# Gated cross-attention stack: the first attention's probabilities turned by VectorE and two DRAM passes instead of by TensorE

## The reference, cut to what matters

```python
q_hk = (hidden_q @ Wq.T).reshape(b, s, H, K)
q_big = jnp.einsum('bshk,hkq->bshq', q_hk, w_kc_q)
kv_rope = kv_c * cos[None] + _rotate_half(kv_c) * sin[None]
q_r = jnp.einsum('bshq,hqr->bhsr', q_big, W_qr)
k_r = jnp.einsum('bld,hdr->bhlr', kv_rope, W_kr)
scores = jnp.einsum('bhsr,bhlr->bhsl', q_r, k_r)
attn = jax.nn.softmax(scores, axis=-1)
ctx_c = jnp.einsum('bhsl,bld->bhsd', attn, kv_rope)
ctx_lat = jnp.einsum('bhsd,hkd->bshk', ctx_c, w_kc_kv)
out = ctx_lat.reshape(b, s, H * K) @ Wo.T
```

## Time and profile before

| what | value |
|---|---|
| median of 3 runs | 1410.36 us (1408.68 to 1412.06) |
| profiled execution, its own time | 1410.01 us |
| its span | 1408.2 us |
| mean granted TensorE clock | 0.998 of full speed |
| PE busy | 1384.4 us, 98% of the span |
| PE weight loads busy | 1128.5 us, 80% |
| DVE busy | 874.9 us, 62% |
| ACT busy | 519.2 us, 37% |
| POOL busy | 404.9 us, 29% |
| DMA moved | 89.07 MB, mean 63 GB/s |

### The profile page before, as it was taken

How to read it: one execution, slowest core, us unless ns; L and a number is a source line. 1 busy time by engine, 2 the same in 40 slices (tenths; PEclk the granted TensorE clock), 3 DMA queues, 4 the chain that set the end, 5 groups by cost and what they waited for, 6 DMA issues and landing times.

```text
span 1408.2 us, 20791 instructions
## 1 busy us (share of the span) xinstructions
PE 1384.4 (98%) x7948; PEld 1128.5 (80%) x7948; DVE 874.9 (62%) x1729; ACT 519.2 (37%) x1599; POOL 404.9 (29%) x463
## 2 busy tenths in 40 slices
PE   6999999999999999999999999999999999999999
PEld 5888888888887788878887888778887788887887
DVE  5455454455554687777677757776788787734443
ACT  2544444444355322131113211321126777822221
POOL 3112322222224444111121112113527865621000
PEclk9999999999999999999999999999999999999999
DMA  5432010110203221111011101111214131132111
GB/s 202 150 108 89 33 66 8 53 39 8 83 24 94 86 74 56 47 31 49 23 38 42 46 17 48 41 45 49 79 50 141 49 128 61 47 113 67 53 46 45
DMA packets 65127, 89.07 MB, mean 63 GB/s; under 512 B 8044, under 2 KB 31724, under 8 KB 65028
## 3 DMA queue, kind: packets, MB, share of 16 engines
q1 hardware_dynamic: 65028, 87.74, 19.5%
HBM read 70.94 MB, written 16.78 MB: 62 GB/s over the span
## 4 chain that ended last, share of the span: by engine, by line
PE 92%; DVE 4%; POOL 1%; ACT 1%; DMA 1%; issue 0%; SPq 0%; DVEq 0%; ACTq 0%; POOLq 0%
PE bank L118 86%; PE bank L121 7%; DVE STG L130 0%; DVE AH L130 0%; DVE st L152 0%; DVE XR L140 0%; DMA STG<-in_WoT_dram 0%; DVE sm L146 0%; DMA XR<-in_x_dram 0%; ACT Pb L124 0%; ACT STG L124 0%; DVE XR L137 0%; POOL XR L137 0%; POOL P L130 0%; DVE MSK L136 0%
## 5 line engine op out<-in xcount | busy, mean ns | idle before, releaser
L118 PE MATMUL bank<-XT,AR 128*128 128x512 f32 x1152 | 280.2, 393 | 0.3 <-DVE AR L130 0.2
L118 PE MATMUL bank<-AR 128*128 128x512 f32 x1056 | 261.5, 397 | 0.9 <-DVE PTV L127 0.7
L118 PEld LDWEIGHTS bank<-XT,AR 128*128 128x128 f32 x1152 | 213.8, 188 | 48.5 <-issue 1.5
L118 PEld LDWEIGHTS bank<-AR 128*128 128x128 f32 x1056 | 193.4, 188 | 46.9 <-DVE PTV L140 2.5
L124 ACT ACTIVATE STG<-bank,b1c 128x512 f32<-128x512 f32 x128 | 88.4, 691 | 379.1 <-PE bank L118 300.6
L118 PE MATMUL bank<-AR,CT 128*128 128x512 f32 x768 | 190.3, 397 | 0.0
L118 PE MATMUL bank<-AR,AH 128*128 128x512 f32 x768 | 187.5, 391 | 0.0
L118 PEld LDWEIGHTS bank<-AR,AH 128*128 128x128 f32 x768 | 143.1, 188 | 30.3 <-issue 1.1
L118 PEld LDWEIGHTS bank<-AR,CT 128*128 128x128 f32 x768 | 142.7, 189 | 30.0 <-issue 0.4
L127 DVE CAST AH<-STG 128x512 fp32r<-128x512 f32 x192 | 91.0, 474 | 118.7 <-PE bank L118 104.4
L127 POOL CAST BA<-STG 128x256 fp32r<-128x256 f32 x64 | 29.6, 463 | 420.7 <-PE bank L118 312.5
(11 more groups left out here) (132 smaller groups left out, 1881.0 us busy)
## 6 DMA issues: line engine op xcount, KB each, us to landing
XR<-scr SPq DMA_DIRECT2D x52, 256.0 KB, 2.8
XR<-in_x_dram SPq DMA_DIRECT2D x32, 256.0 KB, 4.2
scr<-XR SPq DMA_DIRECT2D x32, 256.0 KB, 2.0
STG<-in_Wq_dram SPq DMA_DIRECT2D x8, 512.0 KB, 3.4
STG<-in_WoT_dram SPq DMA_DIRECT2D x8, 512.0 KB, 5.4
STG<-in_W1L_dram SPq DMA_DIRECT2D x16, 256.0 KB, 2.6
STG<-in_W_dram SPq DMA_DIRECT2D x16, 256.0 KB, 2.7
STG<-in_B1T_dram SPq DMA_DIRECT2D x64, 64.0 KB, 1.9
```

The lines of the kernel that those rows point to most:

```text
L118: return self.e.matmul(o, w, x, start=start, stop=stop, skip_group_check=True) if self.e else Nothing()
```

## The change

P of units 0 to 29 is no longer transposed by PE. `by_dma(u)` names those units; units 30 and 31 keep `turn1`.

- DVE `blocks1(u)` transposes `Pb` in 32x32 blocks into a new buffer `PY` (two instructions of 128x512), with the column blocks reordered on the way.
- SP `p_store(u)` writes `PY`, 512 KB, to one of two DRAM scratch arrays; `p_load(u)` waits for that and reads it back in four DMAs of 32 partitions, with runs of 1 KB, into a new buffer `PZ`. `PZ` then holds the whole 128x128 transposes.
- ACT `split1p(u)` writes the high part of `PZ` into `PT` and DVE `split1p(u)` the low part, one instruction of 128x1024 on each in place of two of 128x512 that read PSUM.
- The value product moves one iteration later, to u+3, and is made in halves: first half after `k1`, second half after the second half of an output product. The output products move one iteration later too. The last units are placed so that the schedule from u = 33 on is the old one.
- In SP's list the loads of prepared weights stand two units ahead (`prep_a(u+2)`, `p_load(u-2)`, `prep_b(u+2)`); each still waits for the same event as before. Input loads, stores and `kv_split` are placed anew.

```diff
+            PYZ = sb("PYZ", [128, 2, 1024], F32, st1)
...
+        pscr = [nc.dram_tensor(f"pscr{k}", [128, 1024], F32, kind="Internal").ap() for k in range(2)]
...
+        def by_dma(u):
+            return u < 30
+
+        def blocks_in(t):
+            return t.rearrange("p (n i c) -> p n i c", i=4, c=32)
+
+        def blocks_out(t):
+            return t.rearrange("p (i n c) -> p n i c", i=4, c=32)
...
-                for half in range(2):
+                for half in parts:
...
-                    pe.wait_ge(*ps.drained(("pt", u, 0)))
-                    pe.wait_ge(*ps.drained(("pt", u, 1)))
+                    if by_dma(u):
+                        pe.wait_ge(*pz_ok[u])
+                    else:
+                        pe.wait_ge(*ps.drained(("pt", u, 0)))
+                        pe.wait_ge(*ps.drained(("pt", u, 1)))
...
-                if u >= 3:
-                    wo1(u - 3, 1)
+                if 3 <= u < NU:
+                    pv1(u - 3, (0,))
+                if 4 <= u < NU:
+                    wo1(u - 4, 1)
                 if u + 1 < 8:
                     prep_b(u + 1)
-                if 2 <= u <= NU + 1:
-                    pv1(u - 2)
+                if 3 <= u < NU:
+                    pv1(u - 3, (1,))
...
-                if 1 <= u <= NU:
-                    turn1(u - 1)
+                if 3 <= u < NU:
+                    wo1(u - 3, 0)
+                if u == 31:
+                    wo1(28, 1)
+                    turn1(30)
+                    pv1(29)
+                if u == 32:
+                    wo1(29, 0)
+                    wo1(29, 1)
+                    pv1(30)
+                    turn1(31)
+                    wo1(30, 0)
...
+            def split1p(u):
+                key = "pz", u
+                ac.wait_ge(*d_pz[u, 3])
+                if u:
+                    ac.wait_ge(*ps.full(("pv", u - 1, 1)))
+                hi_of(key, blocks_in(PT[:, 0:1024]), blocks_out(PZ))
...
+            def blocks1(u):
+                for j in range(2):
+                    e.wait_ge(*nm_ok[u, j])
+                    if u:
+                        e.wait_ge(*t_py[u - 1])
+                    e.turn(blocks_out(PY)[:, 4 * j:4 * j + 4], blocks_in(Pb)[:, 4 * j:4 * j + 4]).then_inc(*py_ok.mark((u, j)))
+
+            def split1p(u):
+                lo_of(("pz", u), blocks_in(PT[:, 1024:2048]), blocks_out(PZ), blocks_in(PT[:, 0:1024])).then_inc(*pz_ok.mark(u))
...
-                if 1 <= u <= NU:
+                if 2 <= u < NU:
+                    split1p(u - 2)
+                if 1 <= u < 31:
+                    blocks1(u - 1)
+                if u in (31, 32):
+                    pv1(u - 2)
                     turn1(u - 1)
...
+            def p_store(u):
+                e.wait_ge(*py_ok[u, 1])
+                if u >= 2:
+                    e.wait_ge(*d_pz[u - 2, 3])
+                e.dma(pscr[u % 2], PY).then_inc(*t_py.mark(u))
+
+            def p_load(u):
+                e.wait_ge(*t_py[u])
+                if u:
+                    e.wait_ge(*pz_ok[u - 1])
+                src = pscr[u % 2].rearrange("(j r) (i x) -> i r j x", j=4, i=4)
+                for k in range(4):
+                    e.dma(PZ[32 * k:32 * k + 32, :].rearrange("r (j x) -> r j x", j=4), src[k]).then_inc(*d_pz.mark((u, k)))
...
-                if u + 1 < 8:
-                    prep_a(u + 1)
-                    prep_b(u + 1)
+                if u + 2 < 8:
+                    prep_a(u + 2)
+                if 2 <= u < NU:
+                    p_load(u - 2)
+                if u + 2 < 8:
+                    prep_b(u + 2)
```

More of the change, by code:

```diff
@@ L161, in max_index, with turn @@
         return self.e.max_index(o, m, x) if self.e else Nothing()
+    def turn(self, o, x):
+        return self.e.transpose(o, x) if self.e else Nothing()
     def memset(self, o, v):
@@ L225, in build @@
         w12c = sb("w12c", [128, 2, 4], F32)
+        with ExitStack() as st1:
+            PYZ = sb("PYZ", [128, 2, 1024], F32, st1)
         TM = sb("TM", [128, 4, 512], FR, st12)
@@ L776, in tensor @@
                     ln_turn(*after1(m), p - 3, ring4.next())
-                if 1 <= u <= NU:
-                    turn1(u - 1)
+                if 3 <= u < NU:
[10 more added lines that the diff above has]
+                    wo1(30, 0)
                 if u == 33:
+                    wo1(30, 1)
+                    pv1(31)
                     stA0(0)
-                if 2 <= u <= NU + 1:
-                    wo1(u - 2, 0)
+                    wo1(31, 0)
+                if u == 34:
+                    wo1(31, 1)
                 if u == 33:
@@ L1088, in scores1 @@
                     if u:
-                        ac.wait_ge(*ps.full(("pt", u - 1, j)))
+                        ac.wait_ge(*(py_ok[u - 1, j] if by_dma(u - 1) else ps.full(("pt", u - 1, j))))
                     elif j == 0:
@@ L1578, in vector @@
                     k1(u)
-                if u >= 3 and (u - 3) % 8 == 7:
-                    final1((u - 3) // 8, 2)
-                    final1((u - 3) // 8, 3)
+                if 4 <= u < NU and (u - 4) % 8 == 7:
+                    final1((u - 4) // 8, 2)
+                    final1((u - 4) // 8, 3)
+                if u == 34:
+                    final1(3, 2)
+                    final1(3, 3)
                 if u + 1 < 8:
                     prep_b(u + 1)
-                if 2 <= u <= NU:
-                    pv1(u - 2)
+                if 3 <= u < NU:
+                    pv1(u - 3)
                 if u < NU and p == 7 and m + 1 < NM:
@@ L1598, in vector @@
                     masks_b(0)
-                if 2 <= u <= NU + 1 and (u - 2) % 8 == 7:
-                    final1((u - 2) // 8, 0)
-                    final1((u - 2) // 8, 1)
+                if 3 <= u < NU and (u - 3) % 8 == 7:
+                    final1((u - 3) // 8, 0)
+                    final1((u - 3) // 8, 1)
+                if u == 33:
+                    final1(3, 0)
+                    final1(3, 1)
                 if u == 32:
@@ L1971, in gpsimd @@
                     norm1(u - 1)
-                if 2 <= u <= NU + 1 and (u - 2) % 8 == 7 and (u - 2) // 8 + 1 < NM:
-                    kv_split((u - 2) // 8 + 1)
+                if 3 <= u < NU and (u - 3) % 8 == 7 and (u - 3) // 8 + 1 < NM:
+                    kv_split((u - 3) // 8 + 1)
                 if u < NU and 2 <= p <= 5:
@@ L2149, in sync @@
                     kv_load(m + 1)
-                if 2 <= u < NU and (u - 2) % 8 == 7:
+                if 1 <= u < 31:
+                    p_store(u - 1)
+                if 3 <= u < NU and (u - 3) % 8 == 7:
                     for b in (0, 1):
-                        x_store("fin", 0, (u - 2) // 8, b, ("acc", (u - 2) // 8, b))
+                        x_store("fin", 0, (u - 3) // 8, b, ("acc", (u - 3) // 8, b))
                 if u < NU and p == 7:
```

30 lines of the change are left out of this document (20 added, 10 removed).

## The result

| what | before | after |
|---|---|---|
| median | 1411.14 us (1408.68 to 1412.06, 4 runs) | 1424.47 us (1421.80 to 1425.86, 4 runs) |
| ratio, 95% interval | | 1.0095, 1.0073 to 1.0117 |
| span of the profiled execution | 1408.2 | 1424.0 |

The change costs 13 us, more than the noise: the interval of the ratio leaves out 1. The forecast was a gain of 6, and the range ended at 1421. In the page, parts 1 and 4, PE works 15.1 us less than before and its share of the chain falls from 92% to 78%; DVE, DMA and ACT have the rest; the rows answer to the earlier trace rows.

What follows compares the result with a forecast made beforehand. PE bounds the kernel, busy 1384.4 of 1408.2 us. Terms: 25.5 - 11.4 - 4.0 - 1.3 - 2.1 - 0.7 = 6.0 us gained, so 1410.0 becomes 1404 us; range 1391 to 1421, the forecast's own 1399 to 1408.

Steps and rivals of the forecast that it cites:

- 25.5 us off PE's path: Thirty units lose PE's 8 transposes of P, 0.85 us each: 25.5 us saved, all on PE's path.
- The price of a turn: DVE's block transposes of P: 0.61 us start to start, 1.2 for the two in a unit.
- Rival 2: VectorE becomes the bound between split and next score maximum: at 1.1 us a turn, 16 us, time 1420; chance 0.19.
- Layer-norm units 11.4: Macro tiles 1 to 3, p = 3 to 6: PE stalls because DVE is late, 3.8 us each, 11.4 in all.
- Transfers 0.7: P's DRAM round trip, taken as 7 us, is hidden except at u = 7, 15, 23: 0.7 us allowed in all.
- an ACT that waits for `PZ` in ordinary units: A sign named beforehand that would show the forecast wrong; it expected ACT's `PZ` copy never held by a DMA.
- u = 31, 2.1: The router's product waits for the bank of unit 30's turned P, drained after unit 29's `CT`: 2.1 us lost.
- Iterations 1 and 2, 1.3: Without value product and transposes these iterations cover less of the weight loads: 1.3 us of new wait.
- The units with preparation: u = 3 to 6: PE waits for the first half of `CT`, behind A, 1.0 us each, 4.0 in all.
- "two ahead" moves only their place in SP's list: Prepared weights' loads still wait for the same product, so their earlier place in SP's list costs nothing.
- Rival 3, the ring: P's round trip too long, so from 8.3 us ordinary units run at its pace: 1433 at 10 us; chance 0.12.
- second estimate for the store, 3.2 us: Store of P, 512 KB: 2.0 us fixed plus bytes at 436 GB/s gives 3.2 us; the forecast itself took 2.7.

Runs made afterwards that it cites:

- experiment 4: The change without the store and loads of P, the turned blocks used as they are (attention's values differ): 1424.71 us, ratio 1.0100.
- experiment 5: The change with DVE's list reordered from u = 7 on (`ln_pre`, `ln_norm`, `final1` moved): 1408.19 us, ratio 0.9989 against the kernel before.
- experiments 1 and 2: Each on the change alone: first, input tiles issued earlier in SP's list, 1418.98 us; second, whole value product ahead of `prep_b` in u = 3 to 6, 1415.78 us.
- experiment 7: The change with prepared weights again one unit ahead in SP's list, that part alone undone: 1466.50 us, ratio 1.0393 against the kernel before.
- experiment 1: The change with the next macro tile's input tiles issued earlier, in SP's list alone, for u < 8: 1418.98 us, ratio 1.0066.
- experiment 6: One more unused 128x512 DVE turn in each of 30 units: on the change 1446.29 us, on experiment 5 1419.58 us.
- experiment 9: The change with earlier input loads, whole value product ahead of `prep_b` in u = 3 to 6, and DVE's list reordered: 1394.08 us, ratio 0.9881.

## Why the prediction was wrong

1. **25.5 us off PE's path: right.** Where nothing is late a unit takes 11.6 (forecast 11.7), with layer norm 12.1 (12.1), before 12.6 and 13.0.
2. **The price of a turn: right.** 0.684 us each, and the maximum behind two of them starts 1.22 after the first (257.52 to 258.74; forecast 0.61 start to start, 1.2 for two). The split of 1024 columns took 1.06 on ACT and 1.22 on DVE (1.0 and 1.2). Rival 2's place was right, its price of 1.1 a turn was not.
3. **Layer-norm units 11.4: right. Transfers 0.7: too low, some 2.7. In sum 13.9 for 12.1.** u = 11 to 14: 14.4 12.1 12.5 12.6, forecast 14.5 12.3 12.7 12.7. The transfers show in u = 9, 17, 23 and 25 (13.5, 12.1, 12.9 and 12.8; without them, in experiment 4, 11.6, 11.6, 12.1 and 11.6). ACT waits 2.21 us for `PZ` at u = 9, though the forecast had named an ACT that waits for `PZ` in ordinary units as a sign that it was wrong. What the forecast did not see is that the 11.4 were a matter of order: experiment 5 removed nearly all.
4. **u = 31, 2.1: right**, 2.0.
5. **Iterations 1 and 2, 1.3: right in size, 1.4.** PE waits there for loads of `Wo`, 0.91 at 40.72 and 1.07 at 51.55. Another 2.4 stand before the first scores, where the forecast had no term. A longer wait for the same kind of load, 2.10 against 1.02, is 1.1 of them; that wait varies from 0.49 to 2.34 in the experiments' traces. The rest is not explained.
6. **The units with preparation, "Stall 1.0 in each of u = 3 to 6: 4.0 us": wrong, 24.5.** This is the step that failed. Two causes, about equal (experiments 1 and 2 alone give 5.8 and 7.3 us there), make 18.1 together; the 6.4 left are in u = 3. For the first, I looked for the wait on the output product and found 1.0; in the trace that product starts without one, at 80.23. The second half of the value product comes before it, and takes from the ring of four the bank of the first half, which DVE drains behind G, G and A: 2.0, and 3.7 with the clock. I had laid out the bank ring for the first half in ordinary units only. The 6.4 in u = 3 are, by the traces and not by a run of their own, the first round trip of P: 10.8 us where the forecast had 7, with the short iterations 1 and 2 around it (10.7 and 10.8).
7. **'The weights ... so "two ahead" moves only their place in SP's list ...; nothing': wrong, and the second cause.** The sentence looked at the weights' own release, which is indeed the same. It did not ask what stands *behind* them in the list: the input loads came behind a wait that lets go one iteration later, 13.7 us. And the other way around it would have cost 42 us not to move them (experiment 7), which the forecast did not see either.
8. **The clock.** The forecast had no term for it. Waits of 6.2, 0.7 and 2.0 us in one unit bring the mean of 60 to 80 us down to 0.68; in experiment 1 a wait of 2.0 costs 1.7 more by the clock (u = 5).
9. **Rival 3, the ring: fell as a price on every ordinary unit** (u = 8, 10, 16 and 18 take 11.6), but not wholly: some 2.7 us in u = 8 to 30 are the transfers (experiment 4), the first round trip is what is left in u = 3, and with 0.67 us more in DVE's list the ring binds in more places (experiment 6). The forecast's second estimate for the store, 3.2 us, used a figure that the Trainium skill, "DMA: Bandwidth & Descriptors", Anatomy of one DMA, states for DMAs that GpSimd issues. SP issues them here, and the median store landed in 2.6.
10. **The rule from the Trainium skill, "VectorE: DVE Perf Modes", Rules for kernel authors**, that a 128x128 transpose belongs on TensorE where PSUM will do. The change as made agrees with it, 1424 against 1411, but for another reason than the price of a transpose: with the orders mended the same turns on VectorE make 1392.

The sum by these steps: 25.5 - 13.9 - 24.5 - 3.8 - 2.0 + 2.2 = -16.5, with 0.7 that before had in waits of its own; measured -15.8.

## What to carry to other kernels

When a load is moved in a queue that executes in order, price what stands behind it, not only what it waits for itself; and ask for each new entry that waits, as the store of P here, who needs the transfers after it. When a step is split or moved in a ring of buffers, write out for every step of every kind of iteration whose reader it now waits for, above all in the few odd iterations at the start. A loss of 1% by such a change is not a verdict on its idea: three reorderings without any new work made of +0.95% a gain of 1.2% (experiment 9).

## What the runs showed of the hardware that was not expected

**A short wait can cost more than its length on PE.** A bank wait of 2.01 us in a unit of 17 us is mostly followed by a spell at the 1.2 GHz level: the mean clock of such a unit is 0.92, and it is 3.7 us longer. With the wait gone the clock is 1.00. But not always: in the change the same wait in u = 4 is followed by full speed (the unit's clock 1.00, 20.0 us), in u = 5 by the lower level (0.92, 20.6 us). Six matmuls behind the wait, in u = 4 and then u = 5:

```profile
99.48 0.98 PE L118 MATMUL bank<-PT,AR 128*128 128x256 f32 x6 [2.01 <-DVE CT L130]
118.56 1.65 PE L118 MATMUL bank<-PT,AR 128*128 128x256 f32 x6 [2.01 <-DVE CT L130]
```

What decides between the two is not shown.

**A GpSimd instruction beside a VectorE one that reads two tiles in SBUF.** The group of `rstd` on POOL, one value per partition, before (140 to 440 us) and after (150 to 450 us); the numbers behind the bar are busy us and mean ns of one:

```profile
L130 POOL TENSOR_TENSOR rstd<-ve,mhalf 128x1 f32<-128x1 f32 x12 | 6.6, 551 | 68.2 <-DVE ve L136 68.2
```

```profile
L130 POOL TENSOR_TENSOR rstd<-ve,mhalf 128x1 f32<-128x1 f32 x12 | 17.5, 1462 | 44.6 <-DVE ve L136 44.6
```

After the change it starts beside DVE's split (`PT<-PYZ,PT`, which now reads SBUF twice, where it read a PSUM bank), and takes 1.46 us instead of 0.55: at 63.87 it starts 0.16 into the split and ends at 65.33, 0.4 after it. Moved away from the split, in experiment 5, it takes 0.55 again. By the Trainium skill, "SBUF — State Buffer", SBUF: two separate sides, an instruction of VectorE with two inputs in SBUF and one of GpSimd that reads SBUF exclude each other on a shared pair of ports for the whole instruction; the trace agrees.
